# A fused attention and FFN layer: FFN activation and attention output turned in 32x32 blocks on DVE and through device memory, even chunks' output product a step later

## The reference, cut to what matters

```python
q, k = relu(q) + EPS, relu(k) + EPS
k_cumsum = jnp.cumsum(k, axis=2)
context = jnp.cumsum(jnp.einsum('bhnd,bhne->bhnde', k, v), axis=2)
D_inv = 1.0 / jnp.einsum('bhnd,bhnd->bhn', k_cumsum, q)
attn = jnp.einsum('bhnd,bhnde,bhn->bhne', q, context, D_inv)
x = x + attn.transpose(0, 2, 1, 3).reshape(b, n, H * DH) @ Wo + bo
# FFN on layernorm(x), every operand through fp4_quant_dequant (blocks of 16)
h = silu(gate) * y
x = x + fp4_linear(h, w_down)
```

## Time and profile before

| | |
|---|---|
| runs | median 1593.6 us of 3 (1592.9 to 1594.48) |
| profiled execution, its span | 1592.7 us, 0.9 us under that median |
| PE busy | 1575.6 us, 24464 matmuls |
| DVE, ACT, POOL busy | 1118.9, 672.7, 477.8 us |
| DMA | 26.82 MB, mean 17 GB/s |

### The profile page before, as it was taken

One profiled execution on the slowest core, in us unless ns is written; L12 is line 12 of the kernel. 1 busy time (PEld: TensorE's weight loads), 2 busy tenths in 40 slices (PEclk: granted clock), 3 DMA queues, 4 the chain that ended last, 5 costly groups with the idle time before them and its releaser, 6 DMA issues.

```text
span 1592.7 us, 55490 instructions
## 1 busy us (share of the span) xinstructions
PE 1575.6 (99%) x24464; PEld 1485.6 (93%) x24464; DVE 1118.9 (70%) x2438; ACT 672.7 (42%) x1281; POOL 477.8 (30%) x706
## 2 busy tenths in 40 slices
PE   8999999999999999999999999999999999999998
PEld 6999999999999999999999999999999999999998
DVE  7886766666766667666667666676666666666767
ACT  5444344444444434444344443434434344443433
POOL 3332323323233223232232333222322323322233
PEclk9999999999999999999999999999999999999999
DMA  4100000000000000000000000000000000000000
GB/s 161 33 2 16 16 15 5 15 13 15 15 6 15 12 16 16 15 5 16 12 16 15 6 15 12 16 15 16 5 15 12 16 15 6 15 12 16 9 6 18
DMA packets 22013, 26.82 MB, mean 17 GB/s; under 512 B 1808, under 2 KB 20752, under 8 KB 21776
## 3 DMA queue, kind: packets, MB, share of 16 engines
q1 hardware_dynamic: 21776, 23.27, 4.6%
...
## 4 chain that ended last, share of the span: by engine, by line
PE 94%; DVE 4%; issue 1%; DMA 1%; ACT 0%; SPq 0%; POOL 0%; DVEq 0%; POOLq 0%; ACTq 0%
PE bank L496 66%; PE bank L760 3%; PE bank L629 3%; PE bank L664 3%; PE bank L618 3%; PE bank L580 3%; PE bank L805 3%; PE bank L700 3%; PE bank L727 1%; PE bank L747 1%; PE bank L778 1%; PE bank L602 1%; PE bank L506 1%; DMA qkT<-in_L_attn_Wk 1%; PE bank L739 0%
## 5 line engine op out<-in xcount | busy, mean ns | idle before, releaser
L1011 ACT ACTIVATE qkT<-bank 128x512 f32<-128x512 f32 x256 | 153.0, 599 | 275.9 <-PE bank L496 223.6
L1380 POOL TENSOR_SCALAR qkT<-qkT 128x512 f32<-128x512 f32 x256 | 187.9, 741 | 266.2 <-ACT qkT L1011 266.2
L496 PE MATMUL bank<-xT_hi,wqk_hi 128*128 128x256 f32 x1024 | 213.4, 289 | 0.3 <-DVE wqk_lo L1467 0.3
L496 PE MATMUL bank<-xT_hi,wqk_lo 128*128 128x256 f32 x1024 | 203.1, 279 | 0.0
L496 PE MATMUL bank<-xT_lo,wqk_hi 128*128 128x256 f32 x1024 | 203.1, 279 | 0.0
L1350 POOL TENSOR_TENSOR rstd<-var,minus_half 128x1 f32<-128x1 f32 x64 | 35.6, 556 | 430.3 <-DVE var L1664 430.3
L496 PEld LDWEIGHTS bank<-xT_hi,wqk_hi 128*128 128x128 f32 x1024 | 155.2, 188 | 3.9 <-DVE wqk_lo L1467 0.8
L496 PEld LDWEIGHTS bank<-xT_lo,wqk_hi 128*128 128x128 f32 x1024 | 156.1, 188 | 0.0
L496 PEld LDWEIGHTS bank<-xT_hi,wqk_lo 128*128 128x128 f32 x1024 | 156.0, 188 | 0.0
L1467 DVE TENSOR_TENSOR hqT_lo<-bank,hqT_hi 128x512 fp32r<-128x512 f32 x120 | 63.7, 552 | 118.7 <-ACT hqT_hi L1087 118.7
L1467 DVE TENSOR_TENSOR attnT_lo<-bank,attnT_hi 128x512 fp32r<-128x512 f32 (+1 forms) x128 | 88.0, 689 | 60.8 <-ACT attnT_hi L1078 60.3
...
## 6 DMA issues: line engine op xcount, KB each, us to landing
...
out<-out_sb SPq DMA_DIRECT2D x64, 128.0 KB, 1.7
...
probs<-in_L_attn_Wv SPq DMA_DIRECT2D x1, 512.0 KB, 3.5
k_tok<-in_L_attn_Wv SPq DMA_DIRECT2D x1, 512.0 KB, 6.1
attn<-in_L_attn_Wo SPq DMA_DIRECT2D x1, 512.0 KB, 12.1
x<-in_L_attn_Wo SPq DMA_DIRECT2D x1, 512.0 KB, 13.1
```

The source lines that it names most:

```text
L496: at = pe.matmul(dst, lhs_at(kt), rhs_at(kt), start=first and kt == 0, stop=last and kt == k_tiles - 1)
L1011: act.activation(flat(qkT[:, 2 * m:2 * m + 2, :]), bank[bank_of["qk", c, n]][:], ACT.Relu).then_inc(qk_relu, 1)
L1380: pool.tensor_scalar(at, at, QK_EPS, 1.0, ALU.add, ALU.mult).then_inc(qk_ready, 1)
```

## The change

For chunks 4 to 61 `attn`, and for chunks 1 to 58 `hq`, PE no longer transposes. DVE transposes every 32x32 block in place in its own row of blocks (`block_attn`, `block_hq`). SP writes the result to a buffer in device memory (`attn_away`, 512 KB, in three DMAs; `hq_away`, 384 KB, in one) and reads it back in four DMAs, each of which fills 32 partitions, so that the blocks change places too; the second and third write of `attn_away` swap the partition halves of every other 64 columns' pair, as `ident_swapped` did. ACT copies the whole tile as the high part, now from SBUF (`high_sent_attn`, `high_sent_hq`), POOL subtracts for the low part (`low_sent_attn`, `low_sent_hq`). DVE and ACT lose the steps that read the PSUM banks; the bank keys stay. The product of even chunks with Wo moves into the next step behind attend; with it `add_x`, `variance`, `rstd_2`, `normalize_x2`, `begin_x`, `end_x`, `scale_x` of these chunks. The diff, cut:

```diff
+    GROUP = 32
+    GROUPS = P // GROUP
+    SENT_HQ = range(1, END - 3)
+    SENT_ATTN = range(CHUNKS, END)
...
+        hq_blocks = sb("hq_blocks", [P, FPAD])
+        w_square = hq_blocks[:, 0:FFN].bitcast(BF16).rearrange("p (n f) -> p n f", n=2)
...
+        hq_raw = hq[:].rearrange("p (i k c) -> p i k c", i=GROUPS, c=GROUP)
+
+        def by_raw_hq(t):
+            return t[:].rearrange("p k (i c) -> p i k c", c=GROUP)
...
+        def attn_slot(n, kt):
+            return kt % 2 * (KI // 2) + kt // 2 if n in SENT_ATTN else kt
...
+        def is_late(n):
+            return n in SENT_ATTN and n % 2 == 0
+
+        attn_raw = attn[:].rearrange("p (i k c) -> p i k c", i=GROUPS, c=GROUP)
+        attn_blocks = probs[:, 0:INNER].rearrange("p (a o e) -> p a o e", a=GROUPS, o=2)
+
+        def by_raw_attn(t):
+            return t[:].rearrange("p k (i c) -> p i k c", c=GROUP)
+
...
+            def send_hq(n):
+                sp.wait_ge(hq_blocks_ready, sent_hq(n) + 1)
+                if sent_hq(n):
+                    sp.wait_ge(hq_back, 16 * GROUPS * sent_hq(n))
+                sp.dma_start(hq_away, hq_blocks[:]).then_inc(hq_sent, 16)
+
+            def fetch_hq(n):
+                sp.wait_ge(hq_sent, 16 * (sent_hq(n) + 1))
+                at = hq_away.rearrange("(i r) (a e) -> a r i e", r=GROUP, a=GROUPS)
+                for a in range(GROUPS):
+                    sp.dma_start(hq[GROUP * a:GROUP * (a + 1), :].rearrange("r (i e) -> r i e", i=GROUPS), at[a]
+                                 ).then_inc(hq_back, 16)
...
+            def send_attn(n):
+                sp.wait_ge(attn_blocks_ready, sent_attn(n) + 1)
+                if sent_attn(n):
+                    sp.wait_ge(attn_back, 16 * GROUPS * sent_attn(n))
+                to = attn_away.rearrange("p (a o e) -> p a o e", a=GROUPS, o=2)
+                sp.dma_start(to[:, :, 0, :], attn_blocks[:, :, 0, :]).then_inc(attn_sent, 16)
+                for half in range(2):
+                    here, there = (slice(DH * k, DH * (k + 1)) for k in (half, 1 - half))
+                    sp.dma_start(to[there, :, 1, :], attn_blocks[here, :, 1, :]).then_inc(attn_sent, 16)
+
+            def fetch_attn(n):
+                sp.wait_ge(attn_sent, 48 * (sent_attn(n) + 1))
+                at = attn_away.rearrange("(i r) (a e) -> a r i e", r=GROUP, a=GROUPS)
+                for a in range(GROUPS):
+                    sp.dma_start(attn[GROUP * a:GROUP * (a + 1), :].rearrange("r (i e) -> r i e", i=GROUPS), at[a]
+                                 ).then_inc(attn_back, 16)
...
+                if c % 2 == 0:
+                    if g - 3 in SENT_HQ:
+                        send_hq(g - 3)
+                        fetch_hq(g - 3)
+                    if g in SENT_ATTN:
+                        send_attn(g)
+                        fetch_attn(g)
+                else:
+                    if g in SENT_ATTN:
+                        send_attn(g)
+                    if g - 3 in SENT_HQ:
+                        send_hq(g - 3)
+                    if g in SENT_ATTN:
+                        fetch_attn(g)
+                    if g - 3 in SENT_HQ:
+                        fetch_hq(g - 3)
                 if exists(g - 3, ALL_CHUNKS):
                     sp.wait_ge(out_ready, g - 2)
...
-                    if c == 2 and downed:
-                        for n in range(2):
-                            turn_hq(b, c, g - 3, n)
...
+                if is_late(g - 1):
+                    project_out(*divmod(g - 1, CHUNKS), g - 1)
...
-                    if downed and g > 3 and c != 2:
-                        turn_hq(b, c, g - 3, n)
...
-                    turn_attn(b, c, g, n)
+                    if g not in SENT_ATTN:
+                        turn_attn(b, c, g, n)
...
-                project_out(b, c, g)
+                if not is_late(g):
+                    project_out(b, c, g)
...
+            def high_sent_attn(n):
+                act.wait_ge(attn_back, 16 * GROUPS * (sent_attn(n) + 1))
+                act.wait_ge(wo_done, n)
+                act.activation(by_raw_attn(attnT_hi), attn_raw, ACT.Copy).then_inc(attnT_hi_ready, 2)
...
+            def high_sent_hq(n):
+                act.wait_ge(hq_back, 16 * GROUPS * (sent_hq(n) + 1))
+                act.wait_ge(down_done, n)
+                act.activation(by_raw_hq(hqT_hi), hq_raw, ACT.Copy).then_inc(hqT_hi_ready, 2)
...
+                if is_late(g - 1):
+                    high_sent_attn(g - 1)
...
+                        if n == 0 and is_late(g - 1):
+                            normalize_x2(g - 1)
...
+                        if n == 1 and is_late(g - 1):
+                            square_x(g - 1)
+                if c % 2 == 0 and g - 3 in SENT_HQ:
+                    high_sent_hq(g - 3)
                 if g == 3:
                     square_h(0)
...
-                    high_attn(g, half)
+                    if g not in SENT_ATTN:
+                        high_attn(g, half)
+                if c % 2 == 1 and g - 3 in SENT_HQ:
+                    high_sent_hq(g - 3)
...
+                        if n == 5 and c % 2 == 1 and g in SENT_ATTN:
+                            high_sent_attn(g)
...
+            def low_sent_attn(n):
+                pool.wait_ge(attnT_hi_ready, 2 * (n + 1))
+                pool.tensor_tensor(by_raw_attn(attnT_lo), attn_raw, by_raw_attn(attnT_hi).bitcast(F32), ALU.subtract
+                                   ).then_inc(attnT_ready, 2)
...
+            def low_sent_hq(n):
+                pool.wait_ge(hqT_hi_ready, 2 * (n + 1))
+                pool.tensor_tensor(by_raw_hq(hqT_lo), hq_raw, by_raw_hq(hqT_hi).bitcast(F32), ALU.subtract
+                                   ).then_inc(hqT_ready, 2)
...
+                late = is_late(g - 1)
+                if late:
+                    low_sent_attn(g - 1)
...
+                    add_eps(u + 1, 0)
+                    if late:
+                        rstd_2(g - 1)
+                    for n in range(1, 4):
                         add_eps(u + 1, n)
+                    if late:
+                        scale_x(g - 1)
+                    if g - 3 in SENT_HQ:
+                        low_sent_hq(g - 3)
                     if g == 1:
...
+                    if g in SENT_ATTN:
+                        low_sent_attn(g)
...
+                if n == 0 and g - 1 in SENT_ATTN:
+                    dve.wait_ge(attn_sent, 48 * sent_attn(g))
...
+                if half == 0 and g - 1 in SENT_ATTN:
+                    dve.wait_ge(attnT_ready, 2 * g)
...
+            def block_attn(g):
+                dve.wait_ge(attn_ready, 2 * (g + 1))
+                dve.transpose(attn_blocks.rearrange("p a o (k c) -> p o k a c", c=GROUP),
+                              attn[:].rearrange("p (k o a c) -> p o k a c", o=2, a=GROUPS, c=GROUP)
+                              ).then_inc(attn_blocks_ready, 1)
...
+            def block_hq(n):
+                dve.wait_ge(hq_ready, n + 1)
+                if sent_hq(n):
+                    dve.wait_ge(hq_sent, 16 * sent_hq(n))
+                dve.transpose(hq_blocks[:].rearrange("p (a k c) -> p k a c", a=GROUPS, c=GROUP),
+                              hq[:].rearrange("p (k a c) -> p k a c", a=GROUPS, c=GROUP)
+                              ).then_inc(hq_blocks_ready, 1)
...
+                if c % 2 == 0 and g - 3 in SENT_HQ:
+                    block_hq(g - 3)
                 if c % 2 == 0:
                     low_x(c, u + 1)
...
+                if g in SENT_ATTN:
+                    block_attn(g)
+                if is_late(g - 1):
+                    add_x(g - 1)
+                    variance(g - 1)
+                if c % 2 == 1 and g - 3 in SENT_HQ:
+                    block_hq(g - 3)
+                if is_late(g - 1):
+                    begin_x(g - 1)
...
-                add_x(g)
+                if not is_late(g):
+                    add_x(g)
```

More of the change, by code:

```diff
@@ L1744, in step @@
                 mask(g, 0)
-                if normed:
+                if normed and not is_late(g - 1):
                     variance(g - 1)
@@ L1795, in step @@
                     round_h(0)
-                if downed and g > 3:
-                    for n in range(2):
-                        low_hq(g - 3, n)
                 if not is_step(3):
```

71 lines of the change are left out of this document (45 added, 26 removed).

## The result

The changed kernel takes 1599.05 us (median of 6 runs, 1597.19 to 1603.03) against 1593.72 for the kernel before on the same chip: a ratio of 1.0037, 95% interval 1.0026 to 1.0049. So it is slower, by a little more than the 0.2% that can be told from nothing, where 1537 was forecast. Its profiled execution has a span of 1595.5 us.

A forecast was written before the change was run, and what follows sets the result against it. PE was taken as the bound, busy 1575.6 of 1592.7 us. 1592.7 - 92 of removed work + 35 of new waits = 1536, so 1537 as median; 8 in 10 runs from 1510 to 1588.

The forecast's parts named there:

- the end of the odd chunk's schedule: End of step c = 1: xn ready at 31.9, step ends at 32.2, so no wait of PE, 0.3 us of slack.
- hq's way back: Odd step: SP reads hq four issues after attn, which is back at 21.6; hq is back at 23.1 us.
- wait (4): Step c = 2: POOL's longer list delays scale_h, add_early ends near 8.8 where PE wants it at 8.2: 0.6 us.
- rival C: Odd step's round trip makes the kernel slower; 11 us trips give 1627. Chance 0.12, shared with Rival B beyond no change.
- D: Milder waits from block turns or round trips, 3.5 to 6 us a sequence: 1552 to 1588 us; chance 0.24.
- the credit: PE's removed transposes and switches: 58 x 0.86 for attn and 58 x 0.75 for hq, taken as 92 us.
- The four waits: New waits of PE, 0.75 + 0.65 + 0.4 + 0.6 = 2.4 us a sequence, 35 us over 14.5 sequences.
- (1): Step c = 1: the late product needs bank 7, held by qk tile 0 until ACT's relu: PE stands 0.75 us.
- (3): Step c = 0: block_hq stands on DVE ahead of low_x, on which add_early hangs: 0.4 us of wait.
- (2): Step c = 3: qk tile 1 needs bank 3, freed only by add_x behind normalize and block_attn on DVE: 0.65 us.
- Rival B: DVE block turns at half rate, 2.3 and 1.7 us: 1597, no change. Chance 0.04 shared with rival C's balance point.

The follow-up runs named there:

- Experiment 5: Changed kernel, but in odd steps SP issues hq's four reads ahead of attn's four: 1575.6 us, ratio 0.9887.
- experiment 1: Changed kernel, but in odd steps POOL issues rstd_1 ahead of the subtraction of the odd chunk's attn: 1611.3 us, ratio 1.0114.
- Experiment 9: experiment 3's kernel, with POOL in odd steps also subtracting hq_blocks from itself twice, results unused: 1548.5 us, ratio 0.9714.
- experiment 3: Changed kernel, but in odd steps DVE instead of POOL makes both subtractions, hq's and attn's: 1548.2 us, ratio 0.9716.
- experiments 7: The attn half of the change alone, hq transposed by PE again as in the kernel before: 1569.1 us, ratio 0.9845.
- experiment 6: The hq half of the change alone, attn transposed by PE again as in the kernel before: 1573.7 us, ratio 0.9871.
- Experiment 10: Changed kernel with the late product behind qk tile 1 in c = 1 and add_x ahead of attn's block turn in c = 3: 1613.9 us, ratio 1.0122.
- experiment 11: experiment 3's kernel plus Experiment 10's two edits and, in even steps, block_hq behind low_x and add_late on DVE: 1526.9 us, ratio 0.9589.

## Why the prediction was wrong

**The step that failed** is the end of the odd chunk's schedule: "the step, 30.15 - 1.6 + 2.9 + 0.75, ends at 32.2: no wait, 0.3 us of slack", with xn at 31.9. In the timeline above, counted from 621.98, PE was ready at 32.3, as forecast within 0.1, but xn came at 33.7. The prediction's list against the trace: hq's blocks 16.8 and 16.5; hq back 23.1 and 24.5; hq subtracted 26.0 and 27.4; attn subtracted 29.9 and 30.9; rstd_1 30.8 and 32.6. Two terms were off:

- hq's way back, by 1.4 us. The first store was taken right (18.1, SP's reads start at 18.3), but the four reads of hq are issued only behind attn's four (1.75 us) and take 1.85 to issue and 2.6 more to land. Experiment 5 shows that this order alone is worth 23 us.
- rstd_1, by 0.8 us. The prediction let POOL's subtraction block DVE, and used that for wait (4). It did not turn it round: DVE's `round_h`, held until 652.87, goes first then, and rstd_1 (L1393) takes 1.34 instead of the 0.70 of experiment 1, where it runs undisturbed. Experiment 9 shows the lock in one direction only, but experiment 3's trace shows the other: there rstd_1 stands beside DVE's subtraction, which began first, and ends 0.56 us after it; its mean over the run is 1360 ns, against 713 in experiment 1 and 690 and 737 in experiments 7 and 6.

```profile
632.44 1.59 DVE L1789 TENSOR_TENSOR attnT_lo<-attn,attnT_hi 128x1024 fp32r<-128x1024 f32 x1
632.93 1.66 POOL L1393 TENSOR_TENSOR small<-small 128x2 f32<-128x2 f32 x1
```

Their sum, 2.2, less the slack of 0.3 and 0.4 by which POOL's own subtractions and add_eps were shorter than forecast, is the 1.51 us of wait before c = 2; before c = 0 it is 0.77. In 14 sequences that is the 30.6 us. It is rival C's mechanism, at the place that C named, with trips of ordinary length; C was priced as trips of 11 us. Its mild form, D, had 3.5 to 6 us of waits a sequence, and 4.7 were measured (36.8 + 30.6 over 14.4 sequences); D's time, 1552 to 1588, missed because of the credit.

**The four waits** were right in kind and place. From 100 to 1500 us, 14.4 sequences, (1) to (4) come to 10.0, 7.7, 8.8 and 10.3 us where 10.8, 9.4, 5.8 and 8.6 were forecast. Their sum, 36.8 against 2.4 x 14.4 = 35, is closer than its terms: misses of both signs offset each other, which is luck. The cause given for (3), the block turn ahead of `low_x`, is not enough: in experiment 6 that turn stands in the same place and PE has no row for probs. In the changed kernel DVE's turn in c = 0 starts only at 608.92, 1.6 us into the step, after 1.46 us idle until POOL's `scale_h` (L1429) is done; so (3), like (4), hangs on POOL's longer list. Adding the four was right only for the part of PE's time on which nothing later depends. Experiment 10 shows that (1) and (2) were partly cover for `turn_x`.

**The credit** of 92 us was too large. The busy time fell by 85.5 where PE hardly waits (experiment 11), by 80.1 as the sum of the two halves; taken from the spans with the named waits set aside (7.7 and 1.4 us between 100 and 1500), experiment 11 gives 70.4 + 6.3 = 77. The 85.5 holds missing records: rows released by "issue" are 10.6 us there and 2.0 in the kernel before (150 to 1500), and less these 8.6 it is 77 as well. So 15 us of credit were never there. The row behind it is hq's: 0.75 us a chunk was counted from one group of four, and 32.1 / 58 = 0.55 measured; attn's 0.86 is 0.83. In the changed kernel itself only 72.5 were seen: in the same matmuls PE is busy 13 us longer than in experiment 11. The first group after a wait is 0.05 to 0.1 us longer (`turn_x` 0.66, without a wait 0.60), 4 to 8 us over its 82 waits by my estimate; the one fall of the clock is some 1.6; the rest is open.

So the 60 us between the forecast span of 1536 and 1595.5 divide into 31 for the wait at `turn_x`, 2 for the four waits, 15 of credit that were never there, and some 12 by which PE's work took longer among the waits, which I can explain only in part.

**Right** were: DVE's block turns (1.25 and 0.95 forecast), POOL's subtractions (2.6 and 2.0), and about so a single transfer (2.7 to 2.9 us from issue to landing, where 3.5 for attn and 3.0 for hq stood for a whole leg). A leg of four issues was not: hq's read leg took 4.4 us, from 20.1 to 24.5 in the step.

```profile
L1787 DVE STREAM_TRANSPOSE probs<-attn 128x1024 f32<-128x1024 f32 x58 | 72.2, 1246 | 2.0
L1851 DVE STREAM_TRANSPOSE hq_blocks<-hq 128x768 f32<-128x768 f32 x58 | 56.5, 974 | 45.5 <-POOL hq L1429 45.1 <-issue 0.4
L1441 POOL TENSOR_TENSOR attnT_lo<-attn,attnT_hi 128x1024 fp32r<-128x1024 f32 x58 | 141.1, 2432 | 268.0 <-ACT attnT_hi L1169 268.0
L1453 POOL TENSOR_TENSOR hqT_lo<-hq,hqT_hi 128x768 fp32r<-128x768 f32 x58 | 110.9, 1912 | 103.0 <-ACT hqT_hi L1184 102.7
```

```profile
attn<-attn_away SPq DMA_DIRECT2D x232, 128.0 KB, 2.9
hq_away<-hq_blocks SPq DMA_DIRECT2D x58, 384.0 KB, 2.7
hq<-hq_away SPq DMA_DIRECT2D x232, 96.0 KB, 2.7
attn_away<-probs SPq DMA_DIRECT2D x58, 256.0 KB, 2.7
```

Rival B falls with the first two rows. The durations of single instructions were not the weak point of this forecast; the ends of two chains that met within 0.3 us were, and with them the price of hq's transposes.
